# Flamingo cross-attention block on one Trainium2 core: the context normalised from a transposed second copy, and the weights of the last stage prepared beside the context's projections and kept in DRAM

## The chip, the cores and the metric

The kernel runs on one core of a Trainium2 chip, as one program with three stages. The metric is the device time of one execution in microseconds. Engines are named as the profile names them: PE is TensorE (PEld its weight loads), DVE is VectorE, ACT is ScalarE, POOL is GpSimd, SP is the engine that issues most DMAs. Each engine runs its own list of instructions in order and waits on semaphores for the others.

## The reference, cut to what matters

```python
# x (2, 1024, 512), context (2, 2048, 512), 16 heads of 64
lat = layer_norm(_layernorm(x), ln_lat_g, ln_lat_b)
ctx = layer_norm(context, ln_ctx_g, ln_ctx_b)
q = lat @ Wq                                # Wq 512 x 1024
k, v = split(ctx @ Wkv, 2)                  # Wkv 512 x 2048
k = apply_rope(k, cos, sin)
attn = softmax(clip(q @ k.T * 64**-0.5, -11, 11))      # per head, 1024 x 2048
x = x + tanh(g_xattn) * ((attn @ v) @ Wo + bo)         # Wo 1024 x 512
# int8 feed-forward: y = _layernorm(x)
rhs_scale = max(absmax(rhs, axis=0), 1e-12) / 127      # rhs 512 x 512, a scale per column
q_rhs = clip(round(rhs / rhs_scale), -127, 127)
x = x + tanh(g_ffn) * (q_lhs @ q_rhs) * lhs_scale * rhs_scale
```

## The kernel before

Every float product whose accuracy matters is made of three: each operand is split into a high part (rounded to the type fp32r) and a low part (the rest), and `split_product` adds hi·hi, lo·hi and hi·lo over KT = 4 slices of 128, so 12 matmuls for one 128x512 result.

**Stage 1, `projections`.** Tokens come in chunks of 512: four of x (QCH), numbered n = 0 to 3, then eight of the context (CCH), c = 0 to 7. A chunk is loaded into `raw` (two slots) with tokens on partitions. `measure` (DVE: bn_stats, bn_aggr) and `sqrt` (ACT) give mean and deviation of each token, `normalise` (DVE) applies them, `turn` (PE, L678) transposes the chunk in 16 blocks of 128x128 into `turn_ps`, `affine` (ACT, L503) multiplies by the gain and adds the bias while copying it to `tok`, and `tok_split` (DVE, L599 and L602) makes `tok_hi` and `tok_lo`. All this is done one chunk ahead, between the products of the current one. For a chunk of x, PE makes MT = 8 products of q, m = 0 to 7 (g = 8n + m counts them), each copied by ACT (`q_hi`, L525), subtracted by DVE (`q_lo`, L624) and stored by SP in both parts. Product g uses bank g % 4 of `proj_ps`, so PE waits for `q_lo` of g - 4; the copy of g waits for the stores of g - 4. For a chunk of the context the products come in the order k0 v0 k1 v1 k2 v2 k3 v3, each of 24 matmuls in two banks. ACT copies them out, DVE turns k by its rotary table and splits it (L644 to L657, six operations for each k), SP stores the results. `w_stage` holds raw weights until the second chunk of x is done.

The work of `turn` stands in PE's order after m = 3 (m = 4 for n = 0) of a chunk of x, and after v1 of a chunk of the context:

```python
                if j == 1 and ahead:
                    turn(c + QCH + 1, 1 - slot)
```

In the last chunk of the context the order is K_AHEAD, and the third and fourth k and v use `turn_ps` in part.

**Stage 2, `attention`.** 16 pairs of heads; for each, 8 batches (b) of four units. `scores` (PE, L888, 24 matmuls), `exps` (ACT, L966, four activations), `clip` (DVE, L1050, one operation over the batch), `add_probs` (DVE, L1062 and L1066, partial row sums), `values` (PE, L900, 16 matmuls, one batch behind the scores), and `sums` twice a pair (PE, L914). In pairs 0 and 1 the kernel also prepares the last stage: SP loads rhs and Wo in pieces, ACT rounds `wo_hi` (L1004), POOL subtracts `wo_lo` (L1093), DVE quantises rhs in 18 small operations (`quantise_rhs`, L1026 to L1044) behind the batches of pair 0, and in pair 1 PE transposes the integers (`turn_rhs`, L927, after the values of batches 2 and 3 of its loop) and spreads the column scales over the partitions (`spread_scales`, L934), with ACT copying the results.

**Stage 3, `output`.** Per 128 tokens: the product with Wo (L1226), residual, layer norm, int8 quantisation, the product with the integers (L1249), residual.

Of the kernel before, what the change touches and what calls it, by code (L numbers as in the profile page):

```python
# [12 lines left out]
P = 128  # L13
# [26 lines left out]
def flamingo_kernel(  # L40
    nc: bass.Bass,
    x: bass.AP,
    context: bass.AP,
    g_xattn: bass.AP,
# [8 lines left out]
    rhs_t: bass.AP,  # L53
    out: bass.AP,
# [7 lines left out]
    rec_scr = nc.dram_tensor("rec_scr", (ALLPAIRS, 2, 2, CH), F32, kind="Internal").ap()  # L62

    o_scr = nc.dram_tensor("o_scr", (BATCH, INNER, NQ), F32, kind="Internal").ap()

    with ExitStack() as ctx:
# [19 lines left out]
        v_stored = [sem(f"v_stored{i}") for i in range(CT)]  # L86

# [15 lines left out]
        with ExitStack() as stage:  # L103
            projections(nc, stage, x, context, cos_t, sin_t, affines, wq, wkv, q_scr, k_scr, v_scr,
                        ident, ident_bf, ones, eps_col, g_xattn, g_ffn, gates, gate_tanh, w_stage, raw, tok, load_pair,
                        v_stored)

        with ExitStack() as scratch:
            ssb, _, _ = tools(nc, scratch)
            rhs_raw = ssb("rhs_raw", [P, KT, DIM])  # L110
            rhs_int = ssb("rhs_int", [P, KT, DIM], BF16)
            diag = ssb("diag", [P, KT, P])
# [3 lines left out]
        with ExitStack() as stage:  # L116
            attention(nc, stage, load_pair, k_st, q_st, v_st, kqv_in, v_stored, late, ends, gate_tanh, wo, bo, rhs_t,
                      rhs_raw, rhs_int, diag, bo_row, o_scr, ident, ident_bf, ones)
        with ExitStack() as stage:  # L119
            output(nc, stage, x, o_scr, out, late, ends, gate_tanh, ident_bf, eps_col)  # L120

class Late:

    def __init__(self, sb, sem, o_raw, o_out):
# [15 lines left out]
        self.o_hi_made = sem("o_hi_made3")  # L140
        self.sum_copied = sem("sum_copied")
# [91 lines left out]
def projections(nc, ctx, x, context, cos_t, sin_t, affines, wq, wkv, q_scr, k_scr, v_scr,  # L233
                ident, ident_bf, ones, eps_col, g_xattn, g_ffn, gates, gate_tanh, w_stage, raw, tok, load_pair,
                v_stored):
# [31 lines left out]
    rope = sb("rope", [P, 2, 2, CH])  # L267
    proj_ps = ps("proj_ps", [P, 4, CH])
# [28 lines left out]
    WARM_LATE = 10  # L297
    turned = sem("turned")
# [43 lines left out]
    def _(sp):  # L342
        def load_chunk(n, slot, src):
            if not isinstance(n, int) or n >= 2:
                sp.wait_ge(turned, KT * (n - 1))
            sp.dma_start(raw[:, slot, :, :], src.rearrange("(t p) d -> p t d", p=P)).then_inc(raw_in[slot], 16)

# [35 lines left out]

        def chunk_rows(n):
            return x[n * CH:(n + 1) * CH, :] if n < QCH else context[(n - QCH) * CH:(n - QCH + 1) * CH, :]
# [9 lines left out]
        for n in range(QCH):  # L395
            for m in range(MT):
                store_q(n, m)
                if m == 0:
                    load_chunk(n + 2, n % 2, chunk_rows(n + 2))
                if n == 1 and m in (1, 3):  # L400
# [1021 lines left out]
```

## Time and profile before

| | |
|---|---|
| time, median of 3 runs | 1489.73 us (1487.76 to 1489.96) |
| the profiled execution | 1489.53 us |
| its span, first to last instruction | 1487.7 us |
| PE busy | 1458.5 us (98%) |
| DVE busy | 1246.0 us (84%) |
| ACT busy | 706.5 us (47%) |
| POOL busy | 118.7 us (8%) |
| DMA traffic | 195.60 MB, mean 131 GB/s |

The span is the time between the first and the last instruction; the execution's own time is 1.8 us more. A busy PE is one that has a matmul in flight; since matmuls overlap, the distance between the starts of two neighbours is what a matmul costs, and not its duration.

### The profile page before, as it was taken

To read this page: it belongs to the slowest core of one execution; us is meant where nothing else is said; L and a number is where in the kernel's file an instruction comes from. 1 tells how busy PE (TensorE), PEld (TensorE's weight loads), DVE (VectorE), ACT (ScalarE), POOL (GpSimd) and SP (SyncE) were. 2 spreads that over 40 slices of the span, in tenths; PEclk is the share of its full clock that TensorE was granted. 3 is DMA by queue.
4 is the path that set the end of the run, shared out by engine and by line. 5 is a ranking of instruction groups with operands and counts; after the bars stand their busy time and mean duration, and the time that the engine had idled before them with its cause. 6 is when DMAs were issued, how large, how long until landed. Compare 5 with 4: busy or idle time off the path is not lost. (4 is left out here: it accounts for less than half of the span.)

```text
span 1487.7 us, 22575 instructions
## 1 busy us (share of the span) xinstructions
PE 1458.5 (98%) x8090; PEld 886.2 (60%) x8090; DVE 1246.0 (84%) x1108; ACT 706.5 (47%) x823; POOL 118.7 (8%) x71
## 2 busy tenths in 40 slices
PE   8999999999999899999999999999999999999997
PEld 7888888888887344444444444444444444444774
DVE  6756666667655999999999999999999999997997
ACT  4432222222223556565655656565656556564332
POOL 0500000000000300000000000000000000001775
PEclk9999999999999999999999999999999999999998
DMA  7783655555667623523532532541551551402652
GB/s 269 249 260 135 205 170 170 186 157 165 193 172 253 165 48 96 129 60 98 133 70 81 135 92 58 135 101 48 135 127 27 130 134 37 121 16 72 171 169 85
DMA packets 144496, 195.60 MB, mean 131 GB/s; under 512 B 36160, under 2 KB 85312, under 8 KB 138304
## 3 DMA queue, kind: packets, MB, share of 16 engines
q1 hardware_dynamic: 141296, 189.71, 45.3%
q10 hardware_dynamic: 3152, 5.25, 0.9%
q8 instruction: 30, 0.49, 0.1%
q14 instruction: 18, 0.15, 0.0%
HBM read 114.83 MB, written 80.08 MB: 131 GB/s over the span
## 5 line engine op out<-in xcount | busy, mean ns | idle before, releaser
L966 ACT ACTIVATE prob<-score_ps 128x1024 f32<-128x1024 f32 x512 | 483.1, 1032 | 187.1 <-PE score_ps L888 184.3
L900 PE MATMUL value_ps<-prob,v_st 128*64 128x512 f32 x2048 | 468.6, 599 | 4.9 <-DVE prob L1050 4.9
L1066 DVE TENSOR_TENSOR prob_sum<-prob_sum,prob 128x2048 f32<-128x2048 f32 x192 | 446.3, 2325 | 13.6 <-DVE prob L1050 0.2
L888 PE MATMUL score_ps<-q_st,k_st 64*128 64x512 f32 x3072 | 396.7, 403 | 7.9 <-ACT prob L966 5.8
L888 PEld LDWEIGHTS score_ps<-q_st,k_st 64*128 64x128 f32 x3072 | 272.8, 186 | 177.5 <-issue 103.1
L1050 DVE TENSOR_SCALAR prob<-prob 128x4096 f32<-128x4096 f32 x128 | 292.7, 2287 | 41.0 <-ACT prob L966 38.8
L900 PEld LDWEIGHTS value_ps<-prob,v_st 128*64 128x64 f32 x2048 | 135.8, 137 | 272.9 <-issue 265.0
L644 DVE TENSOR_TENSOR k_cos<-k_raw,rope 128x1024 f32<-128x1024 f32 x32 | 39.2, 1225 | 100.0 <-ACT k_raw L548 100.0
L553 ACT ACTIVATE v_out<-proj_ps 128x1024 f32<-128x1024 f32 x31 | 31.9, 1028 | 136.7 <-PE proj_ps L230 136.7
L548 ACT ACTIVATE k_raw<-proj_ps 128x1024 f32<-128x1024 f32 x31 | 31.9, 1029 | 105.1 <-PE proj_ps L230 105.1
L1062 DVE TENSOR_TENSOR prob_sum<-prob 128x2048 f32<-128x2048 f32 x32 | 75.8, 2368 | 1.8 <-DVE prob L1050 0.2
L1386 POOL MEMSET unround<- 128x1 f32 x1 | 0.1, 98 | 844.1 <-POOLq L116 844.1
L230 PE MATMUL proj_ps<-tok_hi,wkv_hi 128*128 128x512 f32 x248 | 67.0, 392 | 0.0
L230 PE MATMUL proj_ps<-tok_hi,wkv_lo 128*128 128x512 f32 x248 | 66.3, 389 | 0.0
L230 PE MATMUL proj_ps<-wkv_lo,tok_hi 128*128 128x512 f32 x248 | 66.3, 389 | 0.0
L230 PE MATMUL proj_ps<-wkv_hi,tok_hi 128*128 128x512 f32 x248 | 66.3, 389 | 0.0
L230 PE MATMUL proj_ps<-wkv_hi,tok_lo 128*128 128x512 f32 x248 | 66.3, 389 | 0.0
L230 PE MATMUL proj_ps<-tok_lo,wkv_hi 128*128 128x512 f32 x248 | 66.3, 389 | 0.0
L979 ACT ACTIVATE sum_row<-sum_ps 128x512 f32<-128x512 f32 x32 | 19.2, 599 | 93.4 <-PE sum_ps L914 93.4
L230 PEld LDWEIGHTS proj_ps<-tok_hi,wkv_lo 128*128 128x128 f32 x248 | 46.6, 188 | 9.8
L230 PEld LDWEIGHTS proj_ps<-wkv_hi,tok_hi 128*128 128x128 f32 x248 | 46.6, 188 | 9.7
L230 PEld LDWEIGHTS proj_ps<-tok_lo,wkv_hi 128*128 128x128 f32 x248 | 46.6, 188 | 9.7
(123 smaller groups left out, 1333.6 us busy)
## 6 DMA issues: line engine op xcount, KB each, us to landing
k_st<-k_scr SPq DMA_DIRECT2D x128, 256.0 KB, 6.5
k_scr<-k_hi SPq DMA_DIRECT2D x64, 256.0 KB, 2.7
v_scr<-v_out SPq DMA_DIRECT2D x32, 512.0 KB, 3.4
k_scr<-k_lo SPq DMA_DIRECT2D x64, 256.0 KB, 4.0
q_st<-q_scr SPq DMA_DIRECT2D x16, 1024.0 KB, 10.9
v_st<-v_scr SPq DMA_DIRECT2D x16, 1024.0 KB, 13.8
q_scr<-q_hi SPq DMA_DIRECT2D x32, 256.0 KB, 4.3
q_scr<-q_lo SPq DMA_DIRECT2D x32, 256.0 KB, 4.4
```

Source lines behind the costliest of these rows:

```text
L230: last = pe.matmul(acc, s, m, start=(n == 0), stop=(n == len(terms) - 1))
L548: act.activation(k_raw[:, j % 2, :, :], banks(what, j, order), ACT.Copy).then_inc(k_copied, 1)
L553: act.activation(v_out[:, j, :], banks(what, j, order), ACT.Copy).then_inc(v_copied, 1)
L644: last = dve.tensor_tensor(made[:, :, :], k_raw[:, s, :, :], rope[:, slot, f:f + 1, :].broadcast_to((P, 2, CH)), ALU.mult)
L888: last = pe.matmul(score_ps[:, u % BANKS, a, :], k_st[slot][rows, k_part, s * P:(s + 1) * P], q_st[slot][rows, q_part, cols], start=(t == ...
L900: last = pe.matmul(value_ps[rows, :], v_st[slot][:, s, rows], prob[:, b % 2, i, a * CH:(a + 1) * CH], start=(s == 0), stop=(s == STEPS - 1))
L966: act.activation(prob[:, b % 2, u % BATCH_UNITS, :], score_ps[:, u % BANKS, :, :], ACT.Exp, scale=SCALE).then_inc(exped, 1)
L979: act.activation(late.sum_row[:, :], sum_ps[:, :], ACT.Copy).then_inc(late.sum_copied, 1)
L1050: dve.tensor_scalar(tile, tile, CLIP_LOW, CLIP_HIGH, ALU.max, ALU.min).then_inc(clipped, 1)
L1062: dve.tensor_tensor(total, halves[0], halves[1], ALU.add).then_inc(added, 1)
L1066: dve.tensor_tensor(total, total, halves[j], ALU.add).then_inc(added, 1)
L1386: pool.memset(unround[:, :], -ROUND).then_inc(unround_set, 1)
```

## The change

Context: the host hands over a second copy of the context, each chunk of 512 tokens transposed (`context_t`). Mean and reciprocal deviation are still measured from the plain copy (`measure_rows`, `sqrt_rows`, `invert_rows`), then SP stores these 2x512 numbers to DRAM and reads them back spread over all partitions (`spread_stats`). DVE subtracts and multiplies on the transposed copy (`normalise_columns`), ACT applies gain and bias (`affine_columns`), DVE splits as before. The eight calls of `turn` for chunks of the context are gone; the three for chunks 1 to 3 of x remain. The transposed copy lies in `w_stage`, the spread numbers in `tok`.

Weights of the last stage: the column maxima, scales and inverses of rhs are made during the chunks of x (`rhs_column`, `rhs_scale`); then one eighth of Wo (128 rows) and of rhs (64 rows) is handled at a time, the first piece in the last chunk of x, the others one per chunk of the context: load (`load_piece`), `wo_high` on ACT, `wo_low` and the three operations of `rhs_integers` on DVE, store to DRAM (`store_piece`). rhs is now taken as it lies, so that no transpose is needed. In stage 2 SP loads all of it in `load_prepared`, behind the work for pair 0, PE waits for it in stage 3, and `bo_gated` moves from POOL to ACT in the last pair but one.

```diff
@@ sync, stage 1
+        def spread_stats(c, slot, row):
+            sp.wait_ge(ctx_rstd_made, c + 1)
+            sp.dma_start(stat_scr[bass.ds(row, 2), :].rearrange("f (p t) -> p f t", t=CT), stat[:, slot, :, :]).then_inc(stat_stored, 16)
+            sp.wait_ge(stat_stored, 16 * (c + 1))
+            if isinstance(c, int) and c == 0:
+                sp.wait_ge(tok_lo_made, QCH)
+            for f in range(2):
+                sp.dma_start(rows[:, slot, f, :], stat_scr[bass.ds(row + f, 1), :].broadcast_to((P, CH))).then_inc(rows_in[slot], 16)
+        def load_piece(i, wo_row, rhs_row):
+            if isinstance(i, int) and i == 0:
+                sp.wait_ge(turned, KT * QCH)
+            else:
+                sp.wait_ge(rhs_made, i)
+            sp.dma_start(wo_raw, wo[bass.ds(wo_row, P), :]).then_inc(wo_in, 16)
+            sp.dma_start(rhs_raw[rhs_part, :], rhs[bass.ds(rhs_row, RHS_ROWS), :]).then_inc(rhs_in, 16)
@@ sync, chunks of x
-                if m == 0:
+                if m == 0 and n + 2 < QCH:
                     load_chunk(n + 2, n % 2, chunk_rows(n + 2))
+                if m == 0 and n + 2 >= QCH:
+                    load_rows(n + 2 - QCH, (n + 2 - QCH) * CH)
+                if (n, m) in ((2, 5), (3, 1)):
+                    load_columns(n - 2, n - 2, (n - 2) * CH)
+                if (n, m) in ((0, 3), (1, 0), (1, 4), (2, 0)):
+                    load_rhs_column((0, 1, 3)[n] + (m == 4))
+                if (n, m) == (2, 7):
+                    spread_stats(0, 0, 0)
+                if (n, m) == (3, 3):
+                    load_piece(0, 0, 0)
+                if (n, m) == (3, 7):
+                    store_piece(0, 0, 0)
+                    load_piece(1, P, RHS_ROWS)
@@ sync, chunks of the context
+                if j == 0 and following:
+                    spread_stats(c + 1, 1 - slot, row)
+                    store_piece(c + 1, wo_row[0], rhs_row[0])
+                if j == 0 and ahead:
+                    load_piece(c + 2, wo_row[1], rhs_row[1])
                 if j == 2 and ahead:
-                    load_chunk(c + QCH + 2, slot, context[bass.ds(tok0 + 2 * CH, CH), :])
+                    load_rows(c + 2, tok2)
+                    load_columns(c + 2, slot, tok2)
@@ scalar
+        def affine_columns(c, slot):
+            act.wait_ge(scaled, c + 1)
+            for k in range(KT):
+                act.activation(ctok[slot][:, k, :], ctok[slot][:, k, :], ACT.Identity, bias=gains[:, 3, k:k + 1],
+                               scale=gains[:, 2, k:k + 1]).then_inc(affine_made, 1)
+        def wo_high(i):
+            act.wait_ge(wo_in, 16 * (i + 1))
+            if not (isinstance(i, int) and i == 0):
+                act.wait_ge(ready.wo_stored, 32 * i)
+            act.activation(wo_hi, wo_raw, ACT.Copy).then_inc(wo_hi_made, 1)
@@ scalar, last chunk of x
+                if m == 3 and n + 1 == QCH:
+                    affine_columns(0, 0)
+                if m == 5 and n + 1 == QCH:
+                    wo_high(0)
@@ vector
+        def normalise_columns(c, slot):
+            spread = [rows[:, slot, f:f + 1, :].broadcast_to((P, KT, CH)) for f in range(2)]
+            dve.wait_ge(ctok_in[slot], 16 * (c // 2 + 1))
+            dve.wait_ge(rows_in[slot], 32 * (c // 2 + 1))
+            dve.tensor_tensor(ctok[slot], ctok[slot], spread[0], ALU.subtract).then_inc(centred, 1)
+            dve.wait_ge(centred, c + 1)
+            dve.tensor_tensor(ctok[slot], ctok[slot], spread[1], ALU.mult).then_inc(scaled, 1)
@@ vector, chunks of x
+                if (n, m) in ((0, 7), (1, 2), (1, 6), (2, 2)):
+                    rhs_column((0, 1, 3)[n] + (m == 6))
+                if m == 1 and n + 1 == QCH:
+                    normalise_columns(0, 0)
@@ vector, chunks of the context
                 if j == 0 and ahead:
-                    normalise(c + QCH + 1, 1 - slot)
+                    invert_rows(c + 1, 1 - slot)
+                    wo_low(c + 1)
+                    rhs_integers(c + 1)
                 if j == 1 and ahead:
-                    tok_split(c + QCH + 1, 1 - slot)
+                    normalise_columns(c + 1, 1 - slot)
+                if j == 2 and ahead:
+                    tok_split(c + QCH + 1, 1 - slot, ctok[1 - slot])
@@ tensor, stage 1
-                if m == (4 if n == 0 else 3):
+                if m == (4 if n == 0 else 3) and n + 1 < QCH:
                     turn(n + 1, 1 - slot)
-                if j == 1 and ahead:
-                    turn(c + QCH + 1, 1 - slot)
@@ attention, vector and tensor
-                if first(n):
-                    for k in range(3):
-                        quantise_rhs(3 * b + k)
-                if isinstance(n, int) and n == 1 and b in (2, 3):
-                    turn_rhs(b - 2)
-                if isinstance(n, int) and n == 1 and b == 4:
-                    spread_scales()
```

The order of ACT in the last chunk of x, from the copy of its fourth product to the first copy of the context, before:

```order
L525 ACTIVATE q_hi<-proj_ps 128x512 x5
L503 ACTIVATE tok<-turn_ps,gains 128x512 x4
L525 ACTIVATE q_hi<-proj_ps 128x512 x4
L494 ACTIVATE std<-meanvar,eps_col 128x4
L548 ACTIVATE k_raw<-proj_ps 128x1024
```

and the same stretch of the changed kernel, where `raw<-raw` is `wo_high` (it rounds the piece of Wo that lies in a slot of `raw`):

```order
L673 ACTIVATE q_hi<-proj_ps 128x512 x5
L645 ACTIVATE w_stage<-w_stage,gains 128x512 x4
L673 ACTIVATE q_hi<-proj_ps 128x512 x2
L652 ACTIVATE raw<-raw 128x512
L673 ACTIVATE q_hi<-proj_ps 128x512 x2
L640 ACTIVATE std<-stat,eps_col 128x4
L702 ACTIVATE k_raw<-proj_ps 128x1024
```

The rounding of the first piece of Wo stands between the copies of products 29 and 30.

SP in the last chunk of x, from the first product's stores on, before:

```order
L346 DMA raw<-context_dram 128x4x512
L381 DMA q_scr<-q_hi 128x512
L381 DMA q_scr<-q_lo 128x512
L381 DMA q_scr<-q_hi 128x512
L381 DMA q_scr<-q_lo 128x512
L353 DMA rope<-cos_dram 32x512 x4
L353 DMA rope<-sin_dram 32x512 x4
L381 DMA q_scr<-q_hi 128x512
L381 DMA q_scr<-q_lo 128x512
```

and of the changed kernel, beginning one product earlier, with `spread_stats` ahead of the stores of product 24:

```order
L417 DMA stat_scr<-stat 128x2x4
L422 DMA tok<-stat_scr 128x512 x2
L457 DMA q_scr<-q_hi 128x512
L457 DMA q_scr<-q_lo 128x512
L402 DMA raw<-context_dram 128x2048
L457 DMA q_scr<-q_hi 128x512
L457 DMA q_scr<-q_lo 128x512
L411 DMA w_stage<-context_t_dram 128x4x512
L457 DMA q_scr<-q_hi 128x512
L457 DMA q_scr<-q_lo 128x512
L429 DMA rope<-cos_dram 32x512 x4
```

The stores of product 26 and the rotary table (rope) now stand ahead of the first load of Wo, which follows the stores of product 27.

DVE in a chunk of the context, behind k0, of the changed kernel (`raw<-raw` first is `wo_low`, the three next are `rhs_integers`, `w_stage` is the transposed context):

```order
L766 RECIPROCAL stat<-std 128x4
L791 TENSOR_TENSOR raw<-raw 128x512
L798 TENSOR_TENSOR raw<-raw,inv_row 64x512
L801 TENSOR_SCALAR raw<-raw 64x512
L806 TENSOR_SCALAR rhs_int<-raw 64x512
L873 TENSOR_TENSOR k_cos<-k_raw,rope 128x1024
```

Before, the reciprocal and the four operations of `normalise` (L590) stood there, and `tok_split` behind k1; now `normalise_columns` stands behind k1 and `tok_split` behind k2.

## Rows read from the trace of the kernel before

**Rows 1.** Windows: us, busy us of each engine (instructions), PEclk, DMA share, GB/s.

```profile
112.00:474.00 362.00, 360.79 (x1649) 300.03 (x1647) 238.02 (x312) 88.79 (x103) 0.00 (x0) 1.00 0.57 180
474.00:560.00 86.00, 75.11 (x440) 36.03 (x440) 78.51 (x49) 48.90 (x56) 16.86 (x5) 0.96 0.47 120
```

**Rows 2.** Timeline of PE around one transposed chunk: start, us, instruction.

```profile
133.77 1.91 PE L678 MATMUL turn_ps<-ident,raw 128*128 128x128 f32 x16
...
138.26 1.07 PE L230 MATMUL proj_ps<-tok_hi,wkv_hi 128*128 128x512 f32 x4
...
140.99 1.07 PE L230 MATMUL proj_ps<-wkv_hi,tok_hi 128*128 128x512 f32 x4
```

**Rows 3.** Timeline of PE, first values of pair 0 to pair 1.

```profile
483.15 3.65 PE L900 MATMUL value_ps<-prob,v_st 128*64 128x512 f32 x16 [0.45 <-DVE prob L1050]
...
517.50 4.50 PE L900 MATMUL value_ps<-prob,v_st 128*64 128x512 f32 x16
...
556.93 3.65 PE L900 MATMUL value_ps<-prob,v_st 128*64 128x512 f32 x16
560.52 0.62 PE L927 MATMUL sum_ps<-ident_bf,rhs_int 128*128 128x128 bf16 x8
...
574.91 1.16 PE L934 MATMUL sum_ps<-diag,ones 128*128 128x128 f32 x8
```

**Rows 4.** Timeline of PE in the middle of stage 2.

```profile
900.02 3.65 PE L900 MATMUL value_ps<-prob,v_st 128*64 128x512 f32 x16
...
906.60 3.65 PE L900 MATMUL value_ps<-prob,v_st 128*64 128x512 f32 x16
```

**Rows 5.** Timeline of DVE in pair 0, additions beside POOL and without it.

```profile
505.58 6.68 DVE L1066 TENSOR_TENSOR prob_sum<-prob_sum,prob 128x2048 f32<-128x2048 f32 x2
...
541.13 4.62 DVE L1066 TENSOR_TENSOR prob_sum<-prob_sum,prob 128x2048 f32<-128x2048 f32 x2
```

**Rows 6.** Groups by form: busy us, mean ns, idle before and its releaser.

```profile
L644 DVE TENSOR_TENSOR k_cos<-k_raw,rope 128x1024 f32<-128x1024 f32 x32 | 39.2, 1225 | 100.0 <-ACT k_raw L548 100.0
...
L503 ACT ACTIVATE tok<-turn_ps,gains 128x512 f32<-128x512 f32 x48 | 33.4, 779 | 0.9 <-PE turn_ps L690 0.9
...
L576 DVE BATCH_NORM_STATS2 moments<-raw 128x6 f32<-128x512 f32 x48 | 29.8, 679 | 4.1 <-DMA raw<-x_dram 4.1
L590 DVE TENSOR_SCALAR raw<-raw,meanvar,rstd 128x512 f32<-128x512 f32 x48 | 27.8, 636 | 0.5
L602 DVE TENSOR_TENSOR tok_lo<-tok,tok_hi 128x2048 fp32r<-128x2048 f32 x12 | 27.5, 2292 | 0.4
...
L678 PE MATMUL turn_ps<-ident,raw 128*128 128x128 f32 x176 | 21.0, 272 | 0.0
...
L1026 DVE TENSOR_REDUCE rhs_amax<-rhs_raw 128x1 f32<-128x512 f32 x4 | 2.6, 673 | 0.0
```

**Rows 7.** Timeline of DVE, first and last operation of one k.

```profile
129.59 1.23 DVE L644 TENSOR_TENSOR k_cos<-k_raw,rope 128x1024 f32<-128x1024 f32 x1 [3.02 <-ACT k_raw L548]
...
134.04 1.23 DVE L657 TENSOR_TENSOR k_lo<-k_rot,k_hi 128x1024 fp32r<-128x1024 f32 x1
```

**Rows 8.** DMA issues: count, KB each, median us to landing.

```profile
recip<-rec_scr SPq DMA_DIRECT2D x64, 128.0 KB, 3.1
...
x_in<-x_dram SPq DMA_DIRECT2D x16, 256.0 KB, 4.1
...
rec_scr<-rec_sq SPq DMA_DIRECT2D x32, 4.0 KB, 2.1
```

**Rows 9.** Window of the last chunk of x.

```profile
88.00:112.00 24.00, 24.00 (x115) 20.10 (x114) 10.94 (x16) 7.47 (x12) 0.00 (x0) 1.00 0.79 239
```

**Rows 10.** Timeline of ACT, copies of products 25 and 31.

```profile
94.11 0.60 ACT L525 ACTIVATE q_hi<-proj_ps 128x512 fp32r<-128x512 f32 x1 [2.12 <-PE proj_ps L230]
...
112.20 0.60 ACT L525 ACTIVATE q_hi<-proj_ps 128x512 fp32r<-128x512 f32 x1 [2.12 <-PE proj_ps L230]
```

**Rows 11.** Timeline of SP, half of one rotary table.

```profile
98.72 1.92 SPq L353 DMA_DIRECT2D rope<-cos_dram  x4
```

More of the change, by code:

```diff
@@ L43, in flamingo_kernel @@
     context: bass.AP,
+    context_t: bass.AP,
     g_xattn: bass.AP,
@@ L53, in flamingo_kernel @@
     rhs_t: bass.AP,
+    rhs: bass.AP,
     out: bass.AP,
@@ L592, in normalise, with measure_rows @@
             last.then_inc(normed, 1)
-        def tok_split(n, slot):
+        def measure_rows(c, slot):
+            dve.wait_ge(raw_in[0], 16 * (c + QCH // 2))
+            for t in range(CT):
+                last = dve.bn_stats(moments[:, t, :], raw[:, 0, t, :])
+            last.then_inc(ctx_moments_made, 1)
+            if not (isinstance(c, int) and c < 2):
+                dve.wait_ge(stat_stored, 16 * (c - 1))
+            dve.wait_ge(ctx_moments_made, c + 1)
+            dve.memset(spacer[:, :], 0.0)
+            for t in range(CT):
+                last = dve.bn_aggr(stat[:, slot, :, t], moments[:, t, :])
+            last.then_inc(ctx_aggregated, 1)
@@ L908, in sums @@
                 pe.wait_ge(late.sum_copied, 2 * n + half)
-            if first(n, 2) and not first(n) and half == 0:
-                pe.wait_ge(row_copied, 1)
             for j in range(2):
@@ L916, in sums @@
             last.then_inc(summed, 1)
-        def turn_rhs(part):
-            pe.wait_ge(late.sum_copied, 2)
-            if part == 0:
-                pe.wait_ge(rhs_step, KT + 2 + 3 * KT)
-            else:
-                pe.wait_ge(rhs_copied, 1)
-            for k in range(KT // 2):
-                for t in range(KT):
-                    rows = slice((part * KT // 2 + k) * P, (part * KT // 2 + k + 1) * P)
-                    last = pe.transpose(rhs_ps[:, k, t, :], rhs_int[:, t, rows], ident_bf[:, :])
-            last.then_inc(rhs_turned, 1)
-        def spread_scales():
-            pe.wait_ge(diag_made, KT)
-            pe.wait_ge(rhs_copied, 2)
-            for t in range(KT):
-                last = pe.matmul(row_ps[:, t * P:(t + 1) * P], ones[:, :], diag[:, t, :], start=True, stop=True)
-            last.then_inc(row_made, 1)
         def pair(n, slot):
@@ L1227, in attend @@
                 return last
+            if first(t - 1) and terms:
+                pe.wait_ge(late.prepared_in, 64)
             if terms:
```

287 lines of the change are left out of this document (178 added, 109 removed).

## The prediction

> **What bounds the kernel now.** I first read the windows by stage [rows 1]. In the chunks of the context PE is busy for 360.8 of 362 us at full clock, DVE for 238 and ACT for 89: only what leaves PE's list can shorten this stretch, as long as the others keep up. At the start of stage 2 it is otherwise: PE is busy for 75.1 of 86 us with a mean clock of 0.96, and DVE for 78.5 of the 79 us that follow its first exponentials. There DVE sets the pace.
>
> Then the timeline of PE around a chunk that is transposed [rows 2]. From the first transpose (133.77) to the start 12 matmuls later (138.26) are 4.49 us; the next 12 take 138.26 to 140.99, 2.73 us. So 16 transposes cost 1.77 us of PE (not the 1.91 of their row, which overlaps). A product of k or v is 24 matmuls, 5.45 us, and a chunk eight of these, 43.6 us, or 45.4 with its transposes.
>
> Then PE in stage 2. In its middle one batch takes 906.60 - 900.02 = 6.58 us [rows 4]. From the first values (483.15) to the first `turn_rhs` (560.52) stand ten blocks of values, nine of scores and two of sums [rows 3]: 3.6 + 9 x 6.58 + 2 x 1.0 = 64.8 us if nothing waited (1.0 for a `sums`, eight matmuls like the 1.16 of L934). It took 77.4. So 12.6 us are lost. DVE shows why: two additions take 6.68 us while POOL subtracts a piece of Wo, 4.62 without it [rows 5], and rhs adds small operations such as the four reductions of 0.67 [rows 6]. At 517.50 the same 16 matmuls take 4.50 instead of 3.65 [rows 3]: part of the loss is a clock that fell behind a wait.
>
> **The change, part by part.**
>
> *Transposes.* 176 transposes are 11 chunks of 16 [rows 6]; 8 chunks go: 8 x 1.77 = 14.2 us off PE, which bounds there.
>
> *Start of stage 2.* No POOL, no rounding of Wo, no rhs on DVE. What is left for DVE in a batch is one clip, about as long as an addition (2.3), and two additions, 4.62 [rows 5], 6.9 us, but in two of eight batches one addition fewer: 51 us a pair against PE's 8 x 6.58 + 2 = 54.6. PE becomes the bound as in the later pairs, so I give the whole 12.6 us back. An end below that would be DVE's extra 0.3 us in the first three batches before its short one, plus the filling of the pipeline: 11 us. In pair 1 `turn_rhs` twice and `spread_scales` go, 2 x 0.62 + 1.16 [rows 3] less their overlaps: 2.2 us.
>
> *The later loads.* `load_prepared` moves some 4.9 MB behind the work for pair 0. The queue then moves little else, since the load for pair 3 must wait for the values of pair 1, and the results are wanted in stage 3 only. SP is past the sums and reciprocals of pair 0 by then; those of pair 1 come a batch or more later. I cost it at nothing; without that cover it would hold the sums of one pair for a few us, and DVE has 3 us of slack a pair. `bo_gated` on ACT is one activation of 128x512, hidden.
>
> *Chunks of the context, DVE.* One k takes from 129.59 to 134.04 + 1.23, 5.7 us [rows 7], four of them 22.7. Four bn_stats and their aggregates are 3.3, the split 3.7 (2.29 and two casts) [rows 6]. `normalise` goes, 4 x 0.64 = 2.5. `normalise_columns` adds two operations over 128x2048, 2 x 2.29 = 4.6; `wo_low` and three operations on a 64x512 piece add at most 4 x 0.68, 2.7 (a 128x512 reduction is 0.67) [rows 6]. From 32.2 in 45.4 us to 37.0 in 43.6: still below PE. DVE waited 100.0 us for k_raw in 31 waits [rows 6], 3.2 each, 12.9 a chunk, of which this takes about 5 to 7.
>
> *Chunks of the context, the round trip.* Counting from a chunk's start, k0 is copied at 6.5 and done on DVE at 12.2; SP has stored v0 and k0 at about 13.6, and only then stores the statistics and waits for them. A store of this shape lands in 2.1 us, a spread load of 128 KB in 3.1 [rows 8]; with twice 256 KB behind 1.5 MB of stores I take 8.5 in all: 22. `normalise_columns` stands behind k1, which ends at 23.0. It then ends at 27.6, k2 arrives at 28.3, ACT's four affines (0.78 each [rows 6]) are done at 31.4, k2 ends at 34.0, the split at 37.7, and PE wants it at 43.6. Cover: 6 us. So no wait here. SP itself stands still for the round trip, but the next k is stored at 21.9.
>
> The Trainium skill (DMA: Bandwidth & Descriptors, Specifications) says that runs under 512 B make DMA do a read-modify-write. The statistics are stored in runs of 16 B; the store of the reciprocals has the same runs and lands in 2.1 us [rows 8], so the row speaks against a price.
>
> *Traffic.* 180 GB/s at a share of 0.57 [rows 1] is a capacity of some 315. A chunk moved about 7.5 MB and adds 1 MB of context, 0.5 of spread rows, 0.94 of Wo and rhs: 10 MB in 43.6 us, 230 GB/s, a share of 0.73. Not a bound, but queues get longer.
>
> *The last chunk of x.* Here I expect a new wait. Product 25 is complete at 94.1 and products follow 2.72 us apart [rows 10], so 23 is copied at 88.7. SP comes to `spread_stats(0)` behind its stores at 90 at best; the last rhs column (loaded behind 1 MB, awaited by DVE before the split) makes DVE some us late: I take 92. Round trip in a busy queue (share 0.79 [rows 9]): 7 us, 99. `normalise_columns` 4.6: 103.7, and `q_lo` of 26 is made behind it, 104.4. SP can store 26 only now, then issues a whole rotary table, 2 x 1.92 [rows 11], stores 27, and at 109.2 starts the first load of Wo, behind which ACT waits: 0.5 to issue and 4.1 to land for 256 KB [rows 8], 113.8. Rounding, copy of 30, `q_lo` of 30 are 1.9: 115.6. The first k needs the bank of product 30. PE ends product 31 at 112.2 - 1.8 = 110.4 [rows 10]. PE waits 5.2 us. Both ends: 0 if the round trip and the late DVE cost 5 us less, 9 if as much more. Behind a wait of that kind the clock falls; one such stretch of 3.65 us took 0.85 more [rows 3], and I take two of them, 1.5 us. In the two chunks of x before, the rhs columns may cost PE 0.5 us in all (bounds 0 and 2), since `q_lo` there comes closer to its use.
>
> The Trainium skill (DMA: Bandwidth & Descriptors, Anatomy of one DMA) gives 2.0 us for a DMA and its bytes at 436 GB/s. By an estimate from that page the round trip would be 5.2 instead of 7 and the piece of Wo 2.9 instead of 4.6; PE's wait would be 1.7 and the sum 1464. The rows include queueing in this kernel, so the sum goes by them.
>
> **Sum**, against the profiled execution's 1489.53 us: - 14.2 - 12.6 - 2.2 + 5.2 + 1.5 + 0.5 = - 21.8, so 1467.7; the median of the runs is 0.2 above it. I say 1468.
>
> **Rivals.**
> - *No wait at the end of the x chunks.* For it: four banks and four slots between PE and the stores. Against it: the chain above is serial. 1467.7 - 7.2 = 1460.5; below it only by the half us of the columns.
> - *Every chunk of the context waits a little.* If rows land 8 us later than I think, the split is 2 late, 7 x 2 = 14: 1482. A smaller form, 1 us each, gives 1475. For it: SP stands in the round trip, then in `store_piece`, and traffic grows by a third. Against it: 6 us of cover.
> - *The start of stage 2 gives back only half*, because DVE still does 6.9 us in each of the first full batches and is hardly faster than PE: 1474.
> - *Slower.* The round trip is so slow that each of seven chunks loses more than it gains. 22/7 = 3.1 us a chunk decides: the spread rows would have to land at 31 instead of 22, a round trip of 18 us instead of 8.5. With 20 us it would be 1482 + 14 = 1496. Nothing in rows 8 is near it.
> - *The change does not do what it says*: PE is freed but DVE becomes the bound in the context; 37.0 against 43.6 us speaks against it. It would end like the second rival.
>
> **How the numbers follow.** My forecast (a wait of 3 to 9 us, 1464 to 1472) 0.50; no wait, 1460 to 1464, 0.20; small waits in the context, 1472 to 1483, 0.17; half at the start of stage 2, 1472 to 1476, 0.07; the rest, mostly on the slow side, 0.06. The range 1460 to 1481 leaves out about 1 to 2 in 10. A difference of 0.2% (3 us) is about what can be told from none. Faster: all but the extremes, 0.94; same 0.02; slower 0.04.
>
> **What would show it.** PE without transposes and with chunks of 43.6 us; a gap of about 5 us ahead of the first product with wkv, with ACT idle for `wo_raw` or the copy of product 30 late; in pair 0 blocks of values 6.6 us apart and two additions never above 4.7; no wait of DVE for the spread rows that reaches PE. Wrong would be: chunks longer than 44 us, a PE wait for `tok_hi` at their start, a gap above 9 us at the end of the x chunks, or DVE still at 99% in pair 0 with PE waiting for `prob`.

## The result and the profile after

The changed kernel takes 1477.8 us (median of 6, 1475.15 to 1478.94), the kernel before, run beside it, 1489.64 (1487.58 to 1490.25): a ratio of 0.9922, 95% interval [0.991, 0.9935]. It is faster, as forecast, and inside the range of 1460 to 1481, but by 11.8 us where I forecast 21.8. The time lies outside the 1464 to 1472 of my own case.

First the windows of the changed kernel (us, busy us of each engine with instructions, PEclk, DMA share, GB/s): the end of the x chunks in pieces, then the two stretches of [rows 1].

```profile
84.00:88.00 4.00, 4.00 (x19) 3.30 (x19) 4.00 (x5) 0.60 (x1) 0.00 (x0) 1.00 0.27 99
88.00:92.00 4.00, 4.00 (x20) 3.30 (x19) 3.76 (x12) 1.27 (x3) 0.00 (x0) 1.00 1.04 127
92.00:100.00 8.00, 8.00 (x37) 6.64 (x36) 0.76 (x2) 1.20 (x2) 0.00 (x0) 1.00 0.93 305
100.00:104.00 4.00, 4.00 (x19) 3.11 (x17) 0.00 (x0) 0.60 (x1) 0.00 (x0) 1.00 0.31 41
104.00:112.00 8.00, 0.16 (x1) 0.00 (x0) 4.41 (x2) 0.00 (x0) 0.00 (x0) 0.75 0.97 317
112.00:474.00 362.00, 357.22 (x1556) 295.19 (x1557) 277.92 (x339) 97.67 (x117) 0.00 (x0) 0.99 0.71 238
...
474.00:560.00 86.00, 83.45 (x513) 40.23 (x513) 74.03 (x36) 51.09 (x56) 0.00 (x0) 1.00 0.46 115
```

The last two rows are as forecast: at the start of stage 2 PE is busy for 83.5 us instead of 75.1, at full clock, and DVE is no longer the tighter engine. In the context the queue moves 238 GB/s (my estimate was 230), and PE still bounds. The rows above them are not: from 104 to 112 PE does nothing, and from 88 to 92 the DMA engines are full and yet move only 127 GB/s. From 100 to 104 the queue nearly empties (41 GB/s): SP stands in the round trip until 101.7 and issues nothing.

The timeline of PE there (start, us, instruction, in brackets the idle time before and what ended it):

```profile
103.09 1.07 PE L245 MATMUL proj_ps<-tok_lo,wq_hi 128*128 128x512 f32 x4
112.83 2.08 PE L245 MATMUL proj_ps<-tok_hi,wq_hi 128*128 128x512 f32 x4 [8.68 <-DVE q_lo L839]
114.71 1.91 PE L245 MATMUL proj_ps<-tok_hi,wq_lo 128*128 128x512 f32 x4
116.42 1.91 PE L245 MATMUL proj_ps<-tok_lo,wq_hi 128*128 128x512 f32 x4
118.12 1.15 PE L245 MATMUL proj_ps<-tok_hi,wq_hi 128*128 128x512 f32 x4
...
125.03 1.99 PE L245 MATMUL proj_ps<-tok_hi,wkv_hi 128*128 128x512 f32 x4 [3.94 <-DVE q_lo L839]
126.82 1.86 PE L245 MATMUL proj_ps<-tok_hi,wkv_lo 128*128 128x512 f32 x4
128.52 1.09 PE L245 MATMUL proj_ps<-tok_lo,wkv_hi 128*128 128x512 f32 x4
```

Two waits, 12.6 us, and behind each a slow clock. The granted clock is 0.50 of full speed from 112.83 to 118.12 and 0.51 from 125.03 to 128.52, that is 1.2 GHz instead of 2.4. So the product from 112.83 takes 5.29 us instead of the 2.72 of its neighbours (2.6 lost), and the two groups from 125.03 take 3.49 instead of 1.82 (1.7 lost). From 90 us to the scores these are PE's only waits for a buffer.

The chain behind the first, from the timelines of SP, DVE and ACT:

```profile
93.48 0.44 SPq L417 DMA_DIRECT2D stat_scr<-stat  x1
101.74 0.82 SPq L422 DMA_DIRECT2D tok<-stat_scr  x2
...
107.56 2.29 DVE L773 TENSOR_TENSOR w_stage<-w_stage,tok 128x2048 f32<-128x2048 f32 x1 [12.35 <-DMA tok<-stat_scr]
109.89 2.29 DVE L775 TENSOR_TENSOR w_stage<-w_stage,tok 128x2048 f32<-128x2048 f32 x1
...
112.22 2.93 ACT L645 ACTIVATE w_stage<-w_stage,gains 128x512 f32<-128x512 f32 x4 [10.01 <-DVE w_stage L775]
122.93 0.63 ACT L652 ACTIVATE raw<-raw 128x512 fp32r<-128x512 f32 x1 [6.83 <-DMA raw<-wo_dram]
```

The store of the statistics takes 8.3 us to be seen by SP, the spread rows 5.8 more to release DVE: a round trip of 14.1 us. DVE stands still for 12.35 of it, with `q_lo` of product 26 behind `normalise_columns` in its list; that is what PE waits for. Later ACT waits for the piece of Wo (`raw`), with the copy of product 30 behind it; that is the second wait.

In pair 0 the blocks of values are now 6.65 us apart:

```profile
484.33 3.65 PE L1117 MATMUL value_ps<-prob,v_st 128*64 128x512 f32 x16 [0.45 <-DVE prob L1200]
...
490.98 3.65 PE L1117 MATMUL value_ps<-prob,v_st 128*64 128x512 f32 x16
...
497.62 3.65 PE L1117 MATMUL value_ps<-prob,v_st 128*64 128x512 f32 x16
```

**Where the time went, by stage.** The table divides each profiled execution at three instructions of PE: the first product with wkv, the first scores, the first `wo_ps`. A span is 1.8 to 1.9 us below the time of its own execution. The profiled execution of e12_early_rope is 2.6 us slower than the median of its runs, the others are within 1.3 us of theirs. The experiments below are in the table too.

| kernel | start to first wkv | context, to first scores | stage 2 | stage 3 | span |
|---|---|---|---|---|---|
| before | 112.0 | 362.9 | 894.7 | 118.1 | 1487.7 |
| after | 125.0 | 352.1 | 879.7 | 119.8 | 1476.7 |
| e1_late_wo | 119.2 | 350.5 | 879.8 | 118.2 | 1467.8 |
| e2_early_stats | 120.0 | 352.3 | 879.8 | 119.7 | 1471.9 |
| e3_pool_spread | 123.5 | 350.5 | 879.8 | 119.8 | 1473.5 |
| e4_ctx_only | 112.7 | 351.7 | 893.9 | 118.0 | 1476.3 |
| e5_both | 117.3 | 353.4 | 880.5 | 118.2 | 1469.5 |
| e6_late_inv | 123.2 | 353.0 | 880.8 | 119.8 | 1476.8 |
| e7_no_trip | 121.7 | 352.2 | 880.0 | 119.7 | 1473.5 |
| e8_best | 115.0 | 355.6 | 880.8 | 119.8 | 1471.2 |
| e9_late_scales | 122.7 | 352.9 | 880.7 | 119.8 | 1476.0 |
| e10_early_cols | 122.4 | 351.9 | 879.5 | 119.7 | 1473.5 |
| e11_three | 114.4 | 356.4 | 880.4 | 118.5 | 1469.7 |
| e12_early_rope | 115.4 | 352.0 | 880.9 | 119.7 | 1468.0 |

My forecast, split the same way: +5.4 up to the first wkv (one chunk's transposes off, waits, clock and columns on), -12.4 in the context (seven chunks' transposes), -14.8 in stage 2. Measured: +13.0, -10.8, -15.0, and +1.7 in stage 3. So 7.6 of the missing 10.8 us are lost ahead of the first wkv product, 1.6 in the context, where the slow clock behind the second wait falls (1.7), and 1.7 in stage 3, whose matmuls the change doesn't touch.

### The profile page after: what moved, and what is told of

It is laid out like the page before. It is cut to its first block and busy times, and to the rows that moved or that the text cites. A ratio compares the mean times of both kernels' runs of the same rounds, so it can differ in the third digit from the quotient of the medians.

```text
span 1476.7 us, 22445 instructions
## 1 busy us (share of the span) xinstructions
PE 1444.3 (98%) x7938; PEld 872.4 (59%) x7938; DVE 1268.0 (86%) x1112; ACT 705.0 (48%) x821; POOL 101.8 (7%) x66
## 5 line engine op out<-in xcount | busy, mean ns | idle before, releaser
L1216 DVE TENSOR_TENSOR prob_sum<-prob_sum,prob 128x2048 f32<-128x2048 f32 x192 | 440.1, 2292 | 13.5
L245 PEld LDWEIGHTS proj_ps<-tok_hi,wkv_hi 128*128 128x128 f32 x248 | 46.9, 190 | 14.0 <-issue 4.3
```

The lines of the kernel that those rows point to most:

```text
L245: last = pe.matmul(acc, s, m, start=(n == 0), stop=(n == len(terms) - 1))
L1216: dve.tensor_tensor(total, total, halves[j], ALU.add).then_inc(added, 1)
```

## Experiments

Theory: the loss is the chain at the end of the x chunks, because its transfers land late in a full queue. Rivals: the loss is in what SP or one single transfer does (its waiting, the inverses, the scales, the columns); or it is spread over the context.

**e1_late_wo** moves ACT's and DVE's work on the first piece of Wo behind product 31.

```diff
-                if m == 5 and n + 1 == QCH:
+                if m == 7 and n + 1 == QCH:
                     wo_high(0)
...
-                if n + 1 == QCH and m == 6:
+                if n + 1 == QCH and m == 7:
                     wo_low(0)
-                if n + 1 == QCH and m == 7:
                     rhs_integers(0)
```

> The changed kernel, but the rounding and subtraction of Wo's first piece stand behind the copies of product 31 instead of behind 29 and 30. Theory: the second wait of PE (3.9 us ahead of the first product with wkv) is ACT's wait for that piece, so it goes, with about 1 us of slow clock behind it: 1473 us, and the first wait (8.7 us ahead of product 30) stays as it is. Rival: both waits are one lateness of SP and DVE, and the second only shows where it surfaces next; then the wait moves to another place and the time stays at 1477 to 1478.

Measured 1470.06 us (1469.23 to 1472.6), ratio to before 0.9877 [0.986, 0.9893]. PE's waits from 100 us on:

```profile
PE proj_ps L245 <- DVE q_lo L839: 6.7, 1, 6.7
```

The second wait is gone, with its clock: that the piece of Wo made it is shown. By the trace this is worth 3.9 + 1.7 = 5.6 us, near the 4.8 expected. The time fell by 7.7. The rest isn't the edit's: the first wait is 2.0 us shorter because the store of the statistics goes out at 91.66 instead of 93.48, ahead of everything that was moved, and stage 3 is 1.6 shorter in this execution, for a reason that the next section gives. So some 2 us of the first wait differ from one execution to the next.

**e2_early_stats** makes the first chunk's statistics three products earlier, with their load, and **e5_both** joins it to e1.

```diff
-                if m == 0 and n + 2 >= QCH:
-                    load_rows(n + 2 - QCH, (n + 2 - QCH) * CH)
+                if (n, m) in ((1, 5), (3, 0)):
+                    load_rows(n // 2, (n // 2) * CH)
...
-                if (n, m) == (2, 7):
+                if (n, m) == (2, 4):
                     spread_stats(0, 0, 0)
```

> The changed kernel, but the statistics of the context's first chunk are loaded at product (1,5), measured at (2,2) and spread by SP at (2,4), ahead of the load of the transposed chunk. Theory: PE's wait of 8.7 us was for product 26's low part, which DVE makes behind the spread rows; these now land before DVE asks for them. The wait goes, the chain to the first piece of Wo starts some 8 us earlier and leaves 1 to 2 us of its wait: 1464 to 1467 us. Rival: DMA is simply too full in the chunks of x, so that moving a load of 1 MB to an earlier and fuller place costs PE waits for stored q or late weights there: 1472 or more.

> The moves of the first two experiments together: statistics of the first chunk early, Wo's first piece behind the copies of product 31. Theory: early statistics left waits of 2.0 and 6.6 us, of which the second is the piece of Wo; it goes with its slow clock, so 1466 to 1467 us. Rival: the chunks of x are bound by DMA after all, and q's stores take the place of the piece: 1470 or more.

Measured 1474.74 (1473.8 to 1476.05), ratio 0.9906 [0.989, 0.9923], and 1472.14 (1469.65 to 1473.28), ratio 0.9886 [0.987, 0.9903]. Both miss their theory and land where the rival was put. In e2 PE waits 2.0 and 6.6 us, the second while ACT waits 7.9 us for the piece of Wo. The round trip is off the path: in e5 the store goes out while the queue is nearly idle and is seen 2.1 us later.

```profile
86.99 0.42 SPq L417 DMA_DIRECT2D stat_scr<-stat  x1
89.13 0.81 SPq L422 DMA_DIRECT2D tok<-stat_scr  x2
```

But the rival's wait is there. In e5 the queue is full from 92 to 124 us (windows), and ACT waits for the stores of q. The windows:

```profile
92.00:104.00 12.00, 12.00 (x55) 9.93 (x54) 2.90 (x3) 0.68 (x2) 0.00 (x0) 1.00 1.06 287
104.00:124.00 20.00, 13.47 (x46) 10.30 (x45) 14.10 (x18) 7.04 (x11) 0.00 (x0) 0.83 1.02 360
```

and ACT's waits from 85 to 130 (what it waited for, us in all, times, longest):

```profile
ACT q_hi L673 <- DMA q_scr<-q_lo: 20.0, 6, 6.3
```

PE still waits 6.5 us in two waits, and e5 isn't told apart from e1. With the round trip early, the stores of q in this full stretch hold PE instead.

**e3_pool_spread** gives the first round trip to GpSimd's own queue, so that neither SP nor the stores in its queue stand ahead of it.

```diff
+        pool.dma_start(stat_scr[0:2, :].rearrange("f (p t) -> p f t", t=CT), stat[:, 0, :, :]).then_inc(pool_stored, 16)
+        pool.wait_ge(pool_stored, 16)
+        pool.memset(pool_mark[:, :], 0.0).then_inc(stat_stored, 16)
+        pool.wait_ge(tok_lo_made, QCH)
+        for f in range(2):
+            pool.dma_start(rows[:, 0, f, :], stat_scr[f:f + 1, :].broadcast_to((P, CH))).then_inc(pool_rows, 16)
```

> The changed kernel, but the round trip of the first chunk's statistics alone is issued by GpSimd on its own queue, so that SP does not stand still and the 4 KB store does not queue behind 1 MB and the stores of q. Theory: the store took 8.3 us because of what stood ahead of it; on its own queue it lands in about 3, the rows in 5, PE's first wait shrinks from 8.7 to 0 or 1 us, the second stays at 4 to 5: 1469 to 1471 us. Rival: the landing is slow whatever the queue, since all 16 engines are busy; then the first wait is 6 us or more and the time 1475 or more.

Measured 1475.68 (1475.16 to 1476.44), ratio 0.9911 [0.9894, 0.9928]. The timeline of POOL:

```profile
89.88 0.89 POOL L610 DMA_DIRECT2D stat_scr<-stat  x1 [15.17 <-DVE stat L774]
97.62 0.09 POOL L612 MEMSET pool_mark<- 128x1 f32 x1 [6.86 <-DMA stat_scr<-stat]
```

The store goes out 3.6 us earlier and still takes 7.7 us, and PE waits 8.2 and 2.4 us where 0 to 1 and 4 to 5 were expected. So the order in SP's queue isn't the cause. What the two executions have in common is a full stretch (a DMA share of 0.83 to 1.26 from 88 to 98); that this is the cause is the reading left, and e5's 2.1 us at a share of 0.3 speaks for it.

**e4_ctx_only** keeps the transposed context and leaves the preparation of Wo and rhs in stage 2, as before.

```diff
-                if (n, m) in ((0, 3), (1, 0), (1, 4), (2, 0)):
-                    load_rhs_column((0, 1, 3)[n] + (m == 4))
-                if (n, m) == (2, 4):
-                    store_scales()
...
-                if (n, m) == (3, 3):
-                    load_piece(0, 0, 0)
...
-                    store_piece(c + 1, wo_row[0], rhs_row[0])
```

> Only the transposed context of the change; rhs and Wo are prepared in stage 2 as before. Theory: 14.2 us of transposes go and a round trip of some 13 us costs PE 4 to 5 us ahead of product 30 plus 1.5 of clock (no column of rhs makes DVE late, no piece of Wo is waited for): 1480 to 1482 us. Rival: the wait is made by the weights' extra traffic and work, so this kernel has none: 1475 us. Stage 2 should show the 12.6 and 2.2 us of the kernel before again.

Measured 1478.96 (1478.12 to 1482.71), ratio 0.994 [0.9924, 0.9957]. In the table its first wkv product stands at 112.7 and its context is short, while stage 2 has its 14 us back. So the transposed context alone costs the x chunks 3.8 us of waits in three pieces, no more; the preparation's transfers and work make the other 8.8 us. Its statistics are seen after 5.1 us. The comparison says one thing more: the spans of e4 and of the changed kernel are 1476.3 and 1476.7. The preparation gains 14 us in stage 2 and loses 12.3 of them ahead of the first wkv product; with the 1.8 us of stage 3 nothing is left, and by the medians (1478.96 and 1477.8) about 1 us.

**e6_late_inv** moves the load of the inverses, 256 KB of spread rows that took 8.1 us, from behind product 22 to behind product 28.

```diff
-                if (n, m) == (2, 6):
+                if (n, m) == (3, 4):
                     load_inverses()
```

> The changed kernel, but the load of rhs' inverses, one row of 2 KB spread over 128 partitions, stands at product (3,4) instead of (2,6), behind the statistics' round trip instead of just ahead of it. Theory: between 88 and 92 us the queue is full at 108 to 145 GB/s, and this spread load is what is slow; without it the statistics' store lands in 5 us instead of 8.2, PE's first wait is 5 to 6 us and the time 1474. Rival: the 1 MB of the transposed chunk ahead of it is what it queues behind: 8 us as before, 1477 to 1478.

Measured 1477.26 (1476.47 to 1478.56), ratio 0.992 [0.9903, 0.9936]. The store still takes 8.8 us to be seen (91.35 to 100.11), so the inverses aren't the cause.

**e7_no_trip** spreads two rows of Wo instead of the stored statistics, without waiting for the store. Its context is normalised with other numbers; the loads have the same sizes.

```diff
-            sp.wait_ge(stat_stored, 16 * (c + 1))
...
-                sp.dma_start(rows[:, slot, f, :], stat_scr[bass.ds(row + f, 1), :].broadcast_to((P, CH))).then_inc(rows_in[slot], 16)
+                sp.dma_start(rows[:, slot, f, :], wo[bass.ds(row + f, 1), :].broadcast_to((P, CH))).then_inc(rows_in[slot], 16)
```

> The changed kernel, but the rows that are spread for all eight chunks come from Wo, not from the stored statistics, and SP does not wait for the store; so the context is normalised with other numbers, and the amount of work and traffic is the same. Theory: the 8.3 us in which SP stood still go, rows land before DVE asks or 1 to 2 us after, PE's wait ahead of product 30 goes from 8.7 to 0 to 2 us, that for the piece of Wo stays about 4: 1469 to 1470 us; the chunks of the context do not get shorter, since their round trips were covered. Rival: the chunks of the context hide a loss of their own, then they shorten too and the time is below 1467.

Measured 1475.53 (1474.87 to 1476.32), ratio 0.9911 [0.9894, 0.9927]. I had expected 1469 to 1470, and this fell. The timelines of SP and DVE:

```profile
93.82 1.04 SPq L421 DMA_DIRECT2D tok<-wo_dram  x2
...
104.50 2.29 DVE L772 TENSOR_TENSOR w_stage<-w_stage,tok 128x2048 f32<-128x2048 f32 x1 [9.44 <-DMA tok<-wo_dram]
```

The rows leave 7.9 us earlier and release DVE only 3.1 us earlier; PE waits 5.2 and 3.8 us where 0 to 2 and 4 were expected. In the changed kernel the queue runs dry while SP waits for the store (share 0.03 from 100 to 102). Here SP goes on issuing, and the queue is full until the rows land (share 1.07 from 92 to 104). Of the 14.1 us from the store of the statistics to DVE's release 11.2 remain without the wait between the two transfers: it is what the queue holds, more than the two latencies in a row, that sets the time. The context isn't shorter either (352.2), so the round trip in the seven later chunks costs nothing.

**e8_best** is e5 with the inverses and the second chunk's columns later.

```diff
-                if (n, m) in ((2, 5), (3, 1)):
+                if (n, m) in ((2, 5), (3, 7)):
                     load_columns(n - 2, n - 2, (n - 2) * CH)
```

> Both moves, and rhs' inverses loaded at (3,4), and the second transposed chunk loaded at (3,7) instead of (3,1), so that 1.25 MB leave the fullest stretch of the queue. Theory: PE's waits at the end of the chunks of x are 0 to 2 us: 1462 to 1465 us, that is the 14.2 and 14.8 us of the transposes and of stage 2 nearly whole. Rival: what is left is DVE's lateness by rhs' columns, not the queue; then as with both moves alone, 1466 or 1467.

Measured 1473.11 (1469.15 to 1473.46), ratio 0.9886 [0.9868, 0.9904]: not reached. The two waits shrink to 4.5 us, and a third of 2.9 appears at 129, for the copy of k0, ahead of which ACT waits 7.7 us for the next chunk's statistics and 1.9 for the stores of q.

**e9_late_scales, e10_early_cols, e11_three.** What makes 88 to 92 us so slow? Two transfers stand there, the store of the scales (4 KB in runs of 16 bytes, issued at 86.94) and the load of the first columns (1 MB, at 88.42). e9 moves the one later, with the inverses that need it, e10 the other earlier, and e11 both, on top of e1. (The 8.8 us in the expectation of e9 is e6's; the changed kernel's is 8.3.)

```diff
 # e9
-                if (n, m) == (2, 4):
+                if (n, m) == (3, 4):
                     store_scales()
-                if (n, m) == (2, 6):
+                if (n, m) == (3, 5):
                     load_inverses()
 # e10
-                if (n, m) in ((2, 5), (3, 1)):
+                if (n, m) in ((2, 3), (3, 1)):
```

> The changed kernel, with the store of the rhs scales moved from behind q product 20 to behind product 28, and the load of the inverses behind product 29. In the changed kernel the queue is full (share about 1.0) but moves only 108 to 145 GB/s from 88 to 92 us, where it moves 370 or more at other full places; this stretch begins 1 to 2 us after the store of the scales. Theory A (the store of the scales, in runs of 16 bytes, holds the queue up): the stretch goes, the statistics land in about 5 us instead of 8.8, the rows follow 3 us earlier, PE's first wait falls from 8.7 to about 5.5, time 1474 to 1475. Theory B (the first load of the columns, issued at 88.4, does it): the stretch stays where it is, the statistics still take over 8 us, time 1477 to 1478.

> The changed kernel, with the load of the first chunk's columns moved ahead, from behind product 21 to behind product 19, ahead of the store of the scales. Theory A (the store of the scales makes the stretch of low throughput): the stretch still begins 1 to 2 us after that store and the statistics take over 7 us; time 1476 to 1478. Theory B (the load of the columns makes it): the stretch moves some 4 us ahead with the load, the statistics land in about 5 us, PE's first wait falls to about 5.5, time 1474 to 1475.

> Both moves (scales late, columns early) and the piece of Wo and its rounding behind product 31 as in e1_late_wo, which measured 1470.1. If the landing of the statistics is what the scales or the columns make slow, PE's only wait falls from e1's 6.7 to 3 or less, time 1466 to 1467. If the queue is slow here whatever is issued just before, it stays at 6 to 7 us and the time at 1470.

Measured 1477.5 (1475.52 to 1479.07), 1476.0 (1474.51 to 1477.17) and 1471.64 (1470.53 to 1471.77), ratios 0.9916 [0.99, 0.9933], 0.9909 [0.9892, 0.9925] and 0.9877 [0.986, 0.9893]. Windows, of e9 first:

```profile
88.00:89.40 1.40, 1.40 (x8) 1.17 (x7) 1.40 (x4) 0.00 (x0) 0.00 (x0) 1.00 1.06 364
89.40:91.20 1.80, 1.80 (x10) 1.49 (x9) 1.57 (x9) 0.85 (x3) 0.00 (x0) 1.00 1.00 162
```

and of e10 (columns issued at 81.81, scales at 86.22):

```profile
83.20:84.80 1.60, 1.60 (x9) 1.33 (x8) 1.60 (x1) 0.00 (x0) 0.00 (x0) 1.00 0.84 124
84.80:88.60 3.80, 3.80 (x18) 3.16 (x17) 3.80 (x7) 0.60 (x1) 0.00 (x0) 1.00 1.03 373
88.60:90.40 1.80, 1.80 (x9) 1.50 (x8) 1.56 (x9) 0.78 (x2) 0.00 (x0) 1.00 1.14 178
```

Both theories are half right, by the place of these stretches. Without the scales a stretch of 1.8 us at 162 GB/s is left, 1 us behind the columns; with the columns earlier one such stretch moves with them and one stays some 2 us behind the scales. In the changed kernel, by this reading, the two lie together and make 4 us. Apart, or with one gone, the statistics are seen after 6.8 us (e9), 6.2 (e10) and, with both gone, 4.2 (e11), and the first wait is 5.7, 5.2 and 2.7 us. The landings tell the kernels apart (8.3, 8.3 and 8.8 us in the changed kernel, e1 and e6); of the waits only e11's is clear, since e1 and e6 have 6.7 and 6.8 with both transfers in their old places. The time did not follow in e9: the wait ahead of wkv rose from 3.9 to 5.1, since ACT then waits 7.4 us for the piece of Wo instead of 6.8. In e11 it is only as good as e1, because a wait of 3.0 us appears at 129.5. Its cause is on the timeline of DVE:

```profile
123.75 0.68 DVE L798 TENSOR_TENSOR raw<-raw,inv_row 64x512 f32<-64x512 f32 x1 [4.79 <-DMA inv_row<-scale_scr]
...
127.85 0.28 DVE L761 BATCH_NORM_AGGREGATE stat<-moments 128x2 f32<-128x6 f32 x3
```

DVE stands 4.8 us for the inverses, which now come late; the next chunk's statistics follow, ACT's square root waits for them, and the copy of k0 stands behind it. The late scales took one wait away and made another.

**e12_early_rope** is e11 with both rotary tables loaded where the queue is idle.

```diff
-                if n == 3 and m in (2, 4):
-                    load_rope(m // 2 - 1, m // 2 - 1, (m // 2 - 1) * CH)
+                if n == 0 and m in (4, 5):
+                    load_rope(m - 4, m - 4, (m - 4) * CH)
```

> The kernel of e11_three, with the two rotary tables of the first context chunks (16 issues, 1 MB) loaded behind q products 4 and 5, where the queue stands idle from 42 to 47 us, instead of behind products 26 and 28. Theory: in e11_three SyncE spends 3.7 and 4.0 us on these issues between the stores of q, so that the last stores of q go out some 4 to 8 us late; ACT waits for them with the copy of k0 and PE waits 3.0 us at 129.5 for k0's bank. Without the issues there this wait and the 0.7 ahead of the first product with wkv go, with the clock lost behind them: 1471.6 - 3.7 - 1 = 1467. Rival: the queue itself is full there, the stores land as late as before, and the time stays at 1471 to 1472; or the early loads push the weights of wkv back and the q products wait for them: above 1472.

Measured 1467.31 (1466.72 to 1469.89), ratio 0.9849 [0.9833, 0.9865]. PE's waits from 25 to 135 us:

```profile
PE proj_ps L245 <- DVE q_lo L839: 3.2, 1, 3.2
PE proj_ps L245 <- ACT k_raw L702: 1.1, 1, 1.1
```

It is the best by its runs; its profiled execution is as long as e1's (1468.0 and 1467.8), with 2.3 us less up to the first scores and 2.6 more behind them. The number is as expected, the reason only in part: the copy of k0 didn't wait for the stores of q but, as in e11, for the inverses; they are issued at 118.28 instead of 119.92, since SP no longer spends 7.7 us on 16 issues. DVE still waits 4.67 us for them. With the scales back in their old place and the tables early this wait should go too; that was not run.

## Why the prediction was right in sign and too large in size

That the time fell inside the range is owed to the width of the range. 1477.8 us lies where I had put small waits in the context (1472 to 1483), and those aren't there. What is there is the wait that I forecast, at 12.6 us instead of 5.2, and a gap above 9 us was one of my own signs of being wrong.

- **Transposes, -14.2.** Right. The context lost 10.8 us where seven chunks were to give 12.4, and the difference is the clock behind the second wait; where that wait is absent and none follows (e1) it lost 12.4.
- **Start of stage 2, -12.6 and -2.2.** Right: stage 2 is 15.0 us shorter, and e4, which keeps the old stage 2, has 893.9 of the old 894.7. The additions take 2.29 us each, never more, and the clock is full. The rival that gives half is out.
- **Cover of 6 us in the context.** Right. PE has no wait in chunks 1 to 7; DVE waited for the spread rows 4.1 us in all, in 3 of 7 chunks, and PE didn't notice. The medians over the eight chunks were 3.7 us for the statistics and 4.4 for the rows, near the 8.5 I took. The rivals with 1 or 2 us a chunk, and the slower one, are out; so is DVE as the bound, which is busy for 278 of the 362 us.
- **The later loads.** At no cost, as taken: stage 2 shows none.
- **The new wait.** The mechanism was right link by link (statistics, `normalise_columns`, `q_lo` of 26, a table of issues, the piece of Wo, the copy of product 30), and I had put its upper end at 9 us (which is not the sum I described: 5.2 + 5 is 10.2). The step that failed is its term "Round trip in a busy queue (share 0.79 [rows 9]): 7 us": it was 14.1. The share of 0.79 was that of before [rows 9]; the new transfers of 1 MB, 256 KB and 4 KB stand in just this stretch, where the share was 1.04 for 4 us, at 127 GB/s. The chain ended at 125.0 instead of 115.6, 9.4 us late: 1.5 because the store of the statistics went out at 93.48 and not at 92, 7.1 in the round trip, 0.8 in the rest. That 5.2 + 7 = 12.2 comes so near the 12.6 measured is in part chance, since the late start added to the waits and PE spent 2.6 us of the time at the slow clock and not waiting.
- **The shape of the wait.** I saw one wait ahead of wkv. It came as two, the larger ahead of product 30, since `q_lo` of 26 holds a bank that PE wants 4 products later; so the clock fell twice, and 4.3 us went for it instead of 1.5. (In my own numbers `q_lo` of 26, at 104.4, was only 0.6 us ahead of product 30.)
- **The columns of rhs, 0.5.** They cost PE nothing: it has no wait for a buffer between 30 us and the first of the two.
- **Stage 3, +1.7**, not in my sum. Kernels with the same stage 3 show either 118.0 to 118.5 or 119.7 to 119.8 us. The difference stands in the first row: 2.09 us in before for the first eight `wo_ps` matmuls, 3.42 in the changed kernel. It is TensorE's clock: the granted clock is 0.56 over these eight matmuls in the changed kernel, and 1.00 in the kernel before. It is 1.00 in e1 too, where PE's idle times just ahead (0.5, 1.0 and 1.1 us) are those of the changed kernel. So what makes it fall in one execution and not in another is open; the times of runs can contain it, and up to 2 us between two kernels here say nothing about the edit. Of the two rows that follow, the first is of before, the second of the changed kernel.

```profile
1369.59 2.09 PE L1226 MATMUL wo_ps<-wo_hi,o_hi 128*128 128x512 f32 x8 [0.97 <-PEq L116]
```

```profile
1356.91 3.42 PE L1363 MATMUL wo_ps<-wo_hi,o_hi 128*128 128x512 f32 x8 [1.12 <-PEq L122]
```

The Trainium skill (DMA: Bandwidth & Descriptors, Anatomy of one DMA) fits a DMA issued from GpSimd with 2.0 us and its bytes at 436 GB/s; an estimate from it for the store of 4 KB is 2.0 us. The prediction used the figure for SP's DMAs without saying that it is for GpSimd's. Here SP's store took 2.1 us in a nearly idle queue (e5) and 4.2 to 8.8 in a full one, and GpSimd's own took 7.7 (e3): the fit leaves out what the queue holds.

What is left open: why the first load of columns and the store in 16-byte runs are each followed by about 2 us in which nearly full engines move 120 to 180 GB/s. The Trainium skill (DMA: Bandwidth & Descriptors, Specifications) says that runs under 512 B make DMA read, modify and write. I had let a row of 2.1 us speak against a price; the second stretch of e10 is consistent with a price that the transfers queued beside the store pay, but no run here changes the length of its runs, so it isn't shown. And that rule doesn't cover the stretch behind the columns, whose runs are 2 KB.

## What to carry to other kernels

A round trip through DRAM must be priced with the queue as the change will make it, in the few microseconds where it stands: the mean share of a long window, taken from the kernel before, hid that the new transfers meet there. Small things that somebody waits for (a 4 KB store, a 2 KB row) belong where the queue is idle, and tables that nobody waits for (the rotary ones here) belong away from them; moving the work on one piece of Wo gave back 5.6 us by the trace, the moves of e12_early_rope together some 10. Ask also of each part of a change what it is worth where it is put: the preparation of Wo and rhs was moved out of a stage that it slowed by 14 us, and cost nearly as much in the next full place. And look behind each wait that is taken away: three of these experiments (e5, e8, e11) moved the wait to the next late transfer.

## What the runs showed of the hardware

- **Another queue didn't help** where the engines are full: the 4 KB store took 7.7 us from GpSimd's queue and 8.3 from SP's, one execution of each.
- **A full share isn't full throughput**: 127 GB/s at a share of 1.04 for 4 us, against 373 GB/s at 1.03 right beside such a stretch (e10).
- **The clock behind a wait**: after waits of 8.7 and 3.9 us the granted clock was 0.50, and PE's groups of four matmuls took 1.91 and 1.86 us instead of 1.07, for three groups and for two. That is 2.6 and 1.7 us beside the waits' own length; behind e1's single wait of 6.7 us it was 3.0. The loss didn't grow in step with the wait, so here two waits paid it twice.
- **The length of a wait alone doesn't decide**: behind a wait of 2.7 us the clock stayed at 1.00 for the next product in e5 and was 0.52 over it in e11; behind 3.2 us in e12 it was 1.00 for the first us and 0.60 over the next four.
